# Selective scan: a third decay buffer that lies in SBUF, filled two steps ahead by ScalarE, and normalised rows that share a softplus buffer

## The reference, cut to what matters

```
delta = softplus(...)                       # [channel, time]
dA = jnp.exp(d_t[..., None] * A)            # decay, one row of time for each channel and state
s = s * dA + (d_t * u_t)[..., None] * B_t   # the scan over time
y_t = einsum('bhdn,bhn->bhd', s, C_t)       # sum over the 16 states
```

## Time and profile before

| | |
|---|---|
| time of three runs | 3661.55, 3674.26, 3669.35 us; median 3669.35 |
| the profiled execution | 3666.39 us, its span 3664.2 us |
| busy, share of the span | PE 75%, DVE 62%, POOL 60%, PEld 54%, ACT 43% |
| steps of the selective scan | first scan starts at 2035.19 us, the last at 3064.2 us |

### The profile page before, as it was taken

One profiled execution on the slowest core, in us unless ns is written; L12 is line 12 of the kernel. 1 busy time (PEld: TensorE's weight loads), 2 busy tenths in 40 slices (PEclk: granted clock), 3 DMA queues, 4 the chain that ended last, 5 costly groups with the idle time before them and its releaser, 6 DMA issues. The chain is left out here.

```text
span 3664.2 us, 48790 instructions
## 1 busy us (share of the span) xinstructions
PE 2735.0 (75%) x12964; PEld 1979.9 (54%) x12968; DVE 2264.8 (62%) x4429; ACT 1592.3 (43%) x2930; POOL 2186.9 (60%) x1931
## 2 busy tenths in 40 slices
PE   4699995998479999359994568767867865599910
PEld 4599983444469898348992223322322323589910
DVE  3766653765476565583331798999989897733322
ACT  4433333764443333243333456556546633433300
POOL 0577771222057777345553888988988684455467
PEclk9999996777589999569997799999999997699955
DMA  6011112000401111502232678877877875022322
GB/s 167 11 47 47 47 43 56 25 23 0 121 16 47 45 47 41 156 28 60 70 69 69 225 269 277 266 264 273 275 254 274 280 254 183 23 60 69 70 67 78
DMA packets 287279, 430.20 MB, mean 117 GB/s; under 512 B 58620, under 2 KB 196639, under 8 KB 287168
## 3 DMA queue, kind: packets, MB, share of 16 engines
q1 hardware_dynamic: 251328, 357.61, 29.5%
q0 software_dynamic: 35840, 71.39, 8.1%
HBM read 368.04 MB, written 62.91 MB: 118 GB/s over the span
## 5 line engine op out<-in xcount | busy, mean ns | idle before, releaser
L636 POOL DMA_INDIRECT m_rows<-rows_in,m_source x576 | 561.5, 975 | 366.3 <-PE m_T_ps L664 212.9
L1534 PE MATMUL s_y_ps<-s_prod,ident 128*128 128x512 f32 x1024 | 551.3, 666 | 276.9 <-DVE s_prod L1803 276.6
L1796 DVE TENSOR_TENSOR_SCAN s_dA<-s_dA,s_dBu 128x1024 f32<-128x1024 f32 x256 | 586.3, 2290 | 142.0 <-POOL s_dBu L1494 68.9
L1494 POOL TENSOR_TENSOR s_dBu<-s_du,s_B_row 128x1024 f32<-128x1024 f32 x256 | 603.0, 2359 | 103.0 <-DVE s_dA L1796 95.1
L670 PE MATMUL m_A_ps<-m_rowsT,m_own 128*128 128x256 f32 x2304 | 574.1, 382 | 2.1 <-ACT m_rowsT L718 1.1
L686 PE MATMUL m_Y_ps<-m_own,m_hid 128*128 128x128 f32 x4608 | 562.2, 275 | 3.6 <-issue 3.6
L686 PEld LDWEIGHTS m_Y_ps<-m_own,m_hid 128*128 128x128 f32 x4608 | 537.3, 192 | 5.7 <-issue 5.6
L1534 PEld LDWEIGHTS s_y_ps<-s_prod,ident 128*128 128x128 f32 x1024 | 192.8, 206 | 597.4 <-DVE s_prod L1803 403.6
L670 PEld LDWEIGHTS m_A_ps<-m_rowsT,m_own 128*128 128x128 f32 x2304 | 418.6, 192 | 48.8 <-ACT m_rowsT L718 1.9
L1624 ACT ACTIVATE s_dA<-s_delta,s_decay 128x1024 f32<-128x1024 f32 x256 | 285.5, 1118 | 337.3 <-DVE s_prod L1803 330.6
L728 ACT ACTIVATE m_act_a<-m_A_ps,m_own 128x256 f32<-128x256 f32 x576 | 241.9, 471 | 434.4 <-PE m_A_ps L670 303.2
(11 more groups left out here) (234 smaller groups left out, 4004.8 us busy)
## 6 DMA issues: line engine op xcount, KB each, us to landing
s_B_row<-s_bc_rows SPq DMA_DIRECT2D x256, 512.0 KB, 5.1
s_C_row<-s_bc_rows SPq DMA_DIRECT2D x256, 512.0 KB, 5.4
rows_out<-m_y_sb SPq DMA_DIRECT2D x144, 128.0 KB, 1.8
rows_in<-m_xs SPq DMA_DIRECT2D x64, 256.0 KB, 2.3
m_rows<-rows_in,m_source POOLq DMA_INDIRECT x576, 2.5
s_got<-rows_by_token SPq DMA_DIRECT2D x16, 512.0 KB, 4.8
m_got<-rows_by_token SPq DMA_DIRECT2D x32, 256.0 KB, 4.0
rows_by_token<-m_y_sb,m_target POOLq DMA_INDIRECT x288, 2.3
```

The costliest lines, as they stand in the source:

```text
L636: pool.indirect_dma_start(rows[:, b % 2, r, :], None, c.rows_in, bass.IndirectOffsetOnAxis(source[:, 2 * b + r:2 * b + r + 1], 0)).then_in ...
L1494: nc.gpsimd.tensor_tensor(dBu[q % RING][:, :], du[s % 2][:, h, :], B_row[q % RING][:, :], ALU.mult).then_inc(dBu_ready, 1)
L1534: ins = nc.tensor.matmul(y_ps[:, at(cc, 512)], c.ident[:, :], prod[q % 2][:, at(cc, 512)], start=(n == 0), stop=(n == NS - 1))
L1796: nc.vector.tensor_tensor_scan(dA[q % 2][:, :], dA[q % 2][:, :], dBu[q % RING][:, :], 0.0, ALU.mult, ALU.add).then_inc(scanned, 1)
```

## The change

The pair of `dA` buffers in PSUM gets a third in SBUF. Step q uses buffer `q % 3`, so the steps with q % 3 = 2, 85 of the 256, scan and multiply in SBUF. ACT's `step(q)` issues `decay_of(q + 2)` and still waits for the product of step q - 1. Room for the buffer comes from `xn`, which is now the first half of `e1`, the softplus buffer; the weights that lay there at the start move to the second half; and ACT waits, before it writes `xn`, until POOL has finished the softplus of the sequence before.

```diff
-        xn = sb("xn", [P, TILES, D])
...
-        w_u = e1[:, 0, 0:INNER]
+        w_u = e1[:, 1, 0:INNER]
+        xn = e1[:, 0, :].rearrange("p (j d) -> p j d", d=D)
...
-        dA = [ps(f"dA{i}", SEQ) for i in range(2)]
+        DEPTH = 3
+        dA = [ps(f"dA{i}", SEQ) for i in range(2)] + [sb("dA2", [P, SEQ])]
...
-                wait(act, prod_ready, q - 1)
-                nc.scalar.activation(dA[q % 2][:, :], delta[s % 2][:, h, :], ACT.Exp,
+                wait(act, prod_ready, q - DEPTH + 1)
+                nc.scalar.activation(dA[q % DEPTH][:, :], delta[s % 2][:, h, :], ACT.Exp,
...
                 if t > 0:
                     Use("turned", t - 1, 1).read(act)
+                    act.wait_ge(soft_pool, t * 4 * HALVES)
...
             def step(q):
-                decay_of(q + 1)
+                decay_of(q + DEPTH - 1)
...
-                    decay_of(0)
+                    for q in range(DEPTH - 1):
+                        decay_of(q)
...
-                nc.vector.tensor_tensor_scan(dA[q % 2][:, :], dA[q % 2][:, :], dBu[q % RING][:, :], 0.0,
+                nc.vector.tensor_tensor_scan(dA[q % DEPTH][:, :], dA[q % DEPTH][:, :], dBu[q % RING][:, :], 0.0,
...
-                nc.vector.tensor_tensor(prod[q % 2][:, :], dA[q % 2][:, :], C_row[q % RING][:, :],
+                nc.vector.tensor_tensor(prod[q % 2][:, :], dA[q % DEPTH][:, :], C_row[q % RING][:, :],
```

## The result

The changed kernel takes 3816.23 us (median of 4 runs, 3815.55 to 3822.07), the kernel before, run beside it, 3670.93 us (4 runs, 3661.55 to 3674.26). The ratio is 1.0404, with a 95% interval of 1.0382 to 1.0426: 145 us slower. The profiled span went from 3664.2 to 3814.3 us.

The account below looks back on a forecast made before the run. DVE was taken as fullest, POOL nearly as full. Holding of 179 us less 38 us gained gave +141 on the profiled 3666.4, or 3807 us, rounded to 3808 for the runs' median; range 3715 to 3875.

Parts of the forecast that it names:

- The mechanism: Steps in the SBUF buffer: DVE with two SBUF inputs and POOL hold each other's ports for whole instructions; forecast's chance 0.72.
- The sum of the cost: All 85 steps in SBUF: 46 us plain, 74 us gather and 59 us softplus slots, together 179 us.
- Softplus slots: Slots with two POOL products (27, 28, 29, 31, 0 to 3): 3.0 us per third step, 59 us.
- Gather slots: Slots 5 to 20 of six sequences: DVE's product waits some 2.3 us per third step, 74 us.
- Plain slots: Slots without other POOL work: the scan waits 1.36 us for POOL's product in each third step, 46 us.
- The lead: ACT's decay row one more step ahead: of DVE's 67.0 us of waits, 29.5 stay and about 38 us are gained.
- the wait in slot 29: DVE's 3.35 us wait for ACT per sequence goes, but a wait for POOL's softplus takes its place; no gain.
- The edits at no cost: ACT's added wait before the normalised rows (24 us of cover), its writes to SBUF, loads on SP: claimed to cost nothing.
- rival 1: Only POOL is held, never DVE, so only slots where POOL is the limit pay: +69 us, 3735; chance 0.10.
- rival 3: Ports shared in turns, nothing held for long, ACT's lead counts: 3628 us, at most 3599; chance 0.07.
- rival 2: POOL and DVE hold each other more, also plain slots and gathers: +276 us, 3942, half of it 3880; chance 0.08.
- rival 4: Deeper ring, but waits stay and a third step costs little: within 11 us of before; chance 0.03.

Follow-up runs that it names:

- product_only: Kernel before with shared rows; every third scan reads PSUM but writes SBUF, so only DVE's product has two SBUF inputs: +68.6 us, ratio 1.0180.
- scan_only: Kernel before with shared rows; every third step ACT writes the decay row to SBUF, scan writes PSUM, so only the scan has two SBUF inputs: +110.9 us, ratio 1.0295.
- small_pool_after: Changed kernel with POOL multiplying only 8 of 1024 columns of `dBu`: 3796.48 us; the kernel before, cut the same way, 3797.28 us.
- lead_one: Changed kernel, third buffer kept in SBUF, but ACT one step ahead as before: 3974.36 us, +165.8 against the kernel before, ratio 1.0433.
- one_step: Kernel before with shared rows; only step 10 of each sequence uses an SBUF buffer, ACT two steps ahead for steps 10 to 12: -1.8 us, ratio 0.9994.

## Why the prediction was right, and where it was not

**The mechanism stands.** Two SBUF inputs on DVE beside POOL's work cost the time. product_only and scan_only show that it is the inputs, small_pool_after that it takes a busy POOL, lead_one that the cost is there without the lead. The rule of the Trainium skill (SBUF — State Buffer, Who interferes with whom) by which one side has the shared ports for a whole instruction is borne out in each of the three timelines. Its words on who gets them, whoever issues first, fit the plain slots, where the scan of 2437.65 starts inside POOL's product, but they aren't the whole rule: the scan of 2588.01, in the last section, waited not only for the product under way but for another that started 2 us after the scan. There the measurement decides. The scan of 2395.33 tells less, as a gather was still under way when it started.

**The sum of the cost**: 179 us predicted, 181.0 held in the changed kernel. It is nearly this exact by luck, since its terms are off by more, in both directions, and since 14 us of the 181.0 came with the lead (lead_one has 166.6), which the sum did not foresee. I added up what each instruction lasts above 2.29 or 1.22 us, by slots, over all 256 steps of DVE's timeline:

- Softplus slots: predicted 59 us, measured 61. Some third steps lose 3.0 us, as the one above, some 4.1 (2.16 + 1.96), some 1.96.
- Gather slots: predicted 2.3 us for each and 74 in all; the three-step period of 12.68 us is the 12.7 predicted, but of the 32 third steps there only 14 lose over 2.1 us, ten lose 1.0 to 2.1, and eight nothing: 53 us. Here a step of the prediction was wrong, though the price of a full loss came out. I let the scan start in a gather and have the ports, and the *product* wait for POOL's product, with the gathers free. In the trace it is the *scan* that waits, in 22 of the 32; DVE's product is held in four, in two of them with the scan untouched, as I had it. And the gather is held behind the scan, which the gathers' 60.5 us show; so POOL has less slack than I gave it.
- Plain slots: predicted 1.36 us each, measured 1.20 to 1.22, because the scan is served 0.14 us ahead of the end recorded for POOL's product (its own end at 2441.15, less 2.29, is 2438.86; POOL's product ends at 2439.00). But 67 us in all instead of 46: just beside the softplus slots, in slots 4 and 30 and in slots 5 and 6 of the last two sequences, which I had counted as plain, six steps lose 3.7 to 4.1 us, 23.4 us together, and six steps of slots 21 to 24, just behind the gathers, lose 2.15 to 7.4 us, 20.5 together. At 1.21 us each these twelve would have been 14.5.

**The lead**: predicted +38 us gained, and DVE's waits did fall by 37.5. Without the start of the layer, the idle time before scans and products went from 142.0 - 64.0 + 8.3 = 86.3 us to 85.9 - 66.1 + 26.5 = 46.3, and that before `finish` rose by 2.5. But this total is right with wrong parts. The prediction kept 29.5 us of waits: 2.7 for ACT in slot 10, and 26.8 for POOL in place of the wait in slot 29 (which is before the scan of slot 28, as its start of 2408.70 shows). In the changed kernel none is left for ACT and POOL's grew by 8.9 us only; instead 17.3 us of waits for PE came before products and 2.5 before `finish`. The step that failed is the one that counted waits for ACT as the only thing behind the late bank: PE is held by it too, which one_step shows. The second fault is that lead and holding were added up as if apart. With the lead DVE is held for 14 us more than in lead_one (9 when the changed kernel was run again), and so the lead by itself is worth 20 to 27 us (33 with POOL's products small).

**The edits at no cost** cost 0.1 us.

**The rivals.** That DVE is never held (rival 1) falls with its 181.0 us. That the ports are shared in turns at no price (rival 3) falls with scan_only. Harder mutual holding (rival 2) exists in single cases, which the last section shows, and gathers are held as it said; as the rule for every third step it falls, since most plain slots lose 1.21 us and not 3.7. (Half of it, 3880 us, would have lain above the range, which the prediction says takes it in.) That the change does nothing (rival 4) falls too.

**Left open**: what sets the 145.3 and 139.0 us apart that two groups of runs gave for the same kernel. Their intervals overlap, and the held times (181.0 and 702.4 - 586.3 + 373.0 - 313.2 = 175.9 us) differ by about as much. It is what the gain of the lead is uncertain by.

## What to carry to other kernels

Before a DVE operand goes from PSUM to SBUF beside a busy GpSimd, count the DVE instructions that get a second SBUF input and how much of GpSimd's time lies beside them: here 85 steps cost 166 us, as much as the time for which they were held, where both engines were close to full. When one engine waits for a row that another has queued behind a blocked instruction, look for the event that blocks it and who else is blocked: one number moved by one slot gave 0.7%, a buffer for the one step and a deeper lead there nothing. Price a saved wait together with what the engine meets when it arrives earlier: here 9 to 14 us of the lead's gain went into longer durations. A held instruction shows as a longer duration, not as a wait, so compare shortest, median and longest of each line before and after.

## What the runs showed of the hardware beyond that

A gather, as GpSimd issues it, waits for a DVE scan with two SBUF inputs, and for such a product too: in product_only, where no scan has two, the longest gather took 2.04 us, against 1.05 before. In the kernel before, the 128 gathers took 0.942 to 1.048 us; in the changed kernel:

```profile
L1456 POOL DMA_INDIRECT s_got<-rows_out,s_index x128: 940/987/3075, 1943.5 to 2883.4; - x128
```

And the side that waits isn't always next. The longest product, on the timelines of DVE and of POOL:

```profile
2885.93 8.58 DVE L1806 TENSOR_TENSOR s_prod<-s_dA,s_C_row 128x1024 f32<-128x1024 f32 x1 [0.26 <-DMA s_C_row<-s_bc_rows]
...
2883.43 3.03 POOL L1456 DMA_INDIRECT s_got<-rows_out,s_index  x1 [0.16 <-issue]
2886.48 6.94 POOL L1495 TENSOR_TENSOR s_dBu<-s_du,s_B_row 128x1024 f32<-128x1024 f32 x3
```

DVE's product starts 0.55 us ahead of POOL's first, while a gather is under way, and three of these pass it, until 2893.42; then it takes its 1.2 us. The longest scan shows the same without a gather beside it:

```profile
2588.01 6.55 DVE L1799 TENSOR_TENSOR_SCAN s_dA<-s_dA,s_dBu 128x1024 f32<-128x1024 f32 x1
...
2585.43 6.97 POOL L1495 TENSOR_TENSOR s_dBu<-s_du,s_B_row 128x1024 f32<-128x1024 f32 x3
```

It starts inside the second of three POOL products, and the third, which starts at 2590.05, still goes ahead of it, until 2592.40. In the softplus slots the two engines took turns instead. What decides between the two patterns no run here tells apart; of the 256 steps, three waited for two or more operations of POOL in a row, 15.8 us of the 181.
